# Dense coefficient spreads laid out by GpSimd, and the bias product as steps of the fold's bank rotation

## What is computed

```
x = x + layernorm(x) * scan(0.9, ctx * ctx)          # decayed running sum over tokens
h = layernorm(x) @ W_exp + b_exp                      # 512 -> 2048
h = butterfly(h, up_weights)                          # 11 stages of 2x2 pairs
h = gelu(h + up_bias)
h = butterfly(h, down_weights)
x = x + h @ W_con + b_con + down_bias                 # 2048 -> 512
```

## Time and profile before

| | us |
|---|---|
| median of 3 runs | 2771.31 (2770.5 to 2771.94) |
| profiled execution | 2771.06 |
| its span, first to last instruction | 2769.2 |
| PE busy | 2740.1 (99%) |
| DVE busy | 2122.9 (77%) |
| ACT busy | 1131.0 (41%) |
| GpSimd busy | 396.5 (14%) |

### The profile page before, as it was taken

How to read it: one execution, slowest core, us unless ns; L and a number is a source line. 1 busy time by engine, 2 the same in 40 slices (tenths; PEclk the granted TensorE clock), 3 DMA queues, 4 the chain that set the end, 5 groups by cost and what they waited for, 6 DMA issues and landing times.

```text
span 2769.2 us, 35072 instructions
## 1 busy us (share of the span) xinstructions
PE 2740.1 (99%) x12191; PEld 2260.4 (82%) x12191; DVE 2122.9 (77%) x3554; ACT 1131.0 (41%) x1715; POOL 396.5 (14%) x561
## 2 busy tenths in 40 slices
PE   8899999999999999999999999999999999999998
PEld 6778888888888888888888888888888888888887
DVE  9878787778878777787877878787787877778533
ACT  5743434334343433434343343434434343343432
POOL 4712011110201111010110101011020111102000
PEclk8999999999999999999999999999999999999999
DMA  9795765758576575856757585675857557584543
GB/s 275 266 294 152 216 191 167 228 154 240 165 204 203 168 213 155 255 163 195 201 170 223 155 239 168 190 214 162 235 152 224 185 175 223 161 243 152 182 149 99
DMA packets 292021, 540.48 MB, mean 195 GB/s; under 512 B 36918, under 2 KB 98518, under 8 KB 274950
## 3 DMA queue, kind: packets, MB, share of 16 engines
q1 hardware_dynamic: 285456, 535.77, 64.7%
q10 hardware_dynamic: 5414, 1.25, 0.3%
q0 software_dynamic: 976, 1.22, 0.2%
HBM read 445.83 MB, written 60.82 MB: 183 GB/s over the span
## 4 chain that ended last, share of the span: by engine, by line
PE 98%; ACT 1%; issue 0%; DVE 0%; DMA 0%; ACTq 0%
PE ps L1767 44%; PE ps L1788 25%; PE ps L1801 25%; PE ps L1664 1%; PE ps L1570 1%; PE ps L1642 0%; PE ps L1668 0%; ACT wcon L863 0%; PE ps L1662 0%; ACT w1r L885 0%; PE ps L1670 0%; PE ps L1868 0%; DMA wexp<-in_L_ffn_W_exp_dram 0%; PE ps L1716 0%; PE ps L1589 0%
## 5 line engine op out<-in xcount | busy, mean ns | idle before, releaser
L1767 PE MATMUL ps<-xop,w1r 128*128 128x512 f32 x5376 | 1364.1, 389 | 2.5 <-DVE xop L1296 1.6
L1767 PEld LDWEIGHTS ps<-xop,w1r 128*128 128x128 f32 x5376 | 1008.8, 188 | 212.7 <-DVE xop L1296 2.0
L1788 PE MATMUL ps<-w2r,ghi 128*128 128x512 f32 x2048 | 630.5, 389 | 0.0
L1801 PE MATMUL ps<-w2r,ghi 128*128 128x512 f32 x2032 | 625.8, 389 | 0.0
L1002 ACT ACTIVATE st<-ps 128x512 f32<-128x512 f32 x384 | 229.7, 598 | 839.9 <-PE ps L1767 839.9
L1403 DVE TENSOR_TENSOR x<-ps,x 128x512 f32<-128x512 f32 x508 | 348.6, 686 | 280.6 <-PE ps L1801 278.2
L1788 PEld LDWEIGHTS ps<-w2r,ghi 128*128 128x128 f32 x2048 | 384.4, 188 | 79.8
L1801 PEld LDWEIGHTS ps<-w2r,ghi 128*128 128x128 f32 x2032 | 381.2, 188 | 79.8 <-DVE glo L1426 0.4
L1421 DVE TENSOR_TENSOR g<-ps,st 128x512 f32<-128x512 f32 x384 | 262.9, 685 | 212.5 <-PE ps L1767 212.1
L1006 ACT ACTIVATE g<-g,gelu_bias 128x512 f32<-128x512 f32 x384 | 275.4, 717 | 362.7 <-DVE g L1421 361.6
L1426 DVE TENSOR_TENSOR glo<-g,ghi 128x512 fp32r<-128x512 f32 x510 | 347.5, 702 | 79.9 <-ACT ghi L1020 79.8
(11 more groups left out here) (174 smaller groups left out, 1701.8 us busy)
## 6 DMA issues: line engine op xcount, KB each, us to landing
w1r<-w_products SPq DMA_DIRECT2D x889, 256.0 KB, 3.3
w2r<-w_split SPq DMA_DIRECT2D x126, 1024.0 KB, 5.0
x<-in_x_dram SPq DMA_DIRECT2D x128, 256.0 KB, 7.2
raw<-kv SPq DMA_DIRECT2D x480, 64.0 KB, 2.2
out_dram<-x SPq DMA_DIRECT2D x120, 256.0 KB, 4.0
kv<-in_ctx_dram SPq DMA_DIRECT2D x64, 256.0 KB, 7.3
raw<-in_ctx_dram SPq DMA_DIRECT2D x64, 256.0 KB, 5.3
wexp<-in_L_ffn_W_exp_dram SPq DMA_DIRECT2D x4, 1024.0 KB, 10.9
```

The lines of the kernel that those rows point to most:

```text
L1767: last = nc.tensor.matmul(bank[:, :], w1r[:, slot, w, c * P:(c + 1) * P], xop[:, XPOS[m], v, c, :], start=(opens and i == 0), stop=(i == l ...
L1788: last = nc.tensor.matmul(ps_ya[j][:, :], g[:, p % 2, q, j * P:(j + 1) * P], w2r[:, p % 2, kk, w, :], start=(p == 0 and kk == 0 and i == 0 ...
L1801: last = nc.tensor.matmul(ps_yb[:, :], g[:, p % 2, q, j * P:(j + 1) * P], w2r[:, p % 2, kk, w, :], start=(kk == 0 and i == 0), stop=(kk == ...
```

## The change

It does four things. GpSimd lays the plain and the high coefficients of both sides side by side, one bit after the other (`dense_lows`, `dense_highs`: 4 and 8 copies for each side), and `stage_spread` reads those tiles. The bias turning and the bias product become the FOLD steps "bcol" (behind high_up 11) and "bias_low" (behind high_dn 3), with their evictions in ACT's order. On PE, the parted spreads of the down side go ahead of high_up, the top spread of the down side goes from behind high_up 9 to behind 8, and turn_low becomes plain transposes, its permutation moving into ACT's eviction. On ACT, `square(0, 1)` goes from behind high_up 6 to behind high_up 15, and `weights_hi(0)` gets a target of its own (`w1_first`), so that its wait for the bias product goes and a wait for its store comes in front of the tokens' evictions. On DVE, `high_products(0)` goes ahead of the first statistics.

```
+            def lay_dense(dst, src, order, ready):
+                half_n = dst.shape[1] // 2
+                v = src.rearrange(order, o=KH, a=2, b=2)
+                for bit in range(2):
+                    to = dst[:, bit * half_n:(bit + 1) * half_n]
+                    nc.gpsimd.tensor_copy(to.rearrange("q (o a l) -> q o a l", o=v.shape[1], a=2), v[:, :, :, :, bit])\
+                        .then_inc(ready, 1)
...
             nc.gpsimd.memset(parts_zero(1), 0.0).then_inc(parts_zeroed[1], 1)
+            dense_lows(0)
             load_high(pool, down_w, 1)
...
+            pool.wait_ge(sel_rounded, 2)
+            pool.wait_ge(top_sel_ready, 4)
+            dense_highs(0)
+            pool.wait_ge(fold_made, fold_at("low_up", 3) + 1)
+            dense_lows(1)
+            dense_highs(1)
...
             def weights_hi(n, groups=range(NG)):
                 if n == 0:
-                    act.wait_ge(bias_low, 1)
                     wait_kept(act, "high_up", R - 1)
...
             for r in range(R):
                 fold_step("high_up", r)
+                if r == R - 1:
+                    square(0, 1)
                 if r == 6:
-                    square(0, 1)
                     act.wait_ge(coef_spread, ALL_DONE)
...
-                if r == 13:
-                    act.wait_ge(bcol_turned, 1)
-                    act.activation(bcol, ps[4][:, 256:256 + 2 * KH], ACT.Copy).then_inc(bcol_kept, 1)
+                if r == 11:
+                    fold_step("bcol", 0)
...
-            for r in range(3, 8):
+            fold_step("high_dn", 3)
+            fold_step("bias_low", 0)
+            for r in range(4, 8):
                 fold_step("high_dn", r)
...
+            for group in range(2):
+                act.wait_ge(w1_stored[0][group], NX)
...
+            high_products(0)
             stats1(0, 0, xs[0], range(J))
-            high_products(0)
...
                     for bit in range(2):
                         last = nc.tensor.matmul(ps[bank][:, col:col + n // 2], sel[0:rows, choice, bit, :],
-                                                v[:, :, :, :, bit], start=(bit == 0), stop=(bit == 1))
+                                                dense[:, bit * (n // 2):(bit + 1) * (n // 2)],
+                                                start=(bit == 0), stop=(bit == 1))
...
-                        last = nc.tensor.matmul(o, LX[:, 1, 4 * i + c, :], rank_major(ident[:, :]), start=True, stop=True)
+                        last = nc.tensor.transpose(o, LX[:, 1, 4 * i + c, :], ident[:, :])
...
             spread_high(range(HIGH))
-            spread_low_dn(range(PARTED[0]))
+            spread_low_dn(range(LOWS))
             spread_high_dn(range(HIGH))
...
                 fold_step("high_up", r)
-                if r == 3:
-                    spread_low_dn(PARTED)
-                if r == 9:
+                if r == 8:
                     spread_top_dn((0, 1, 2, 3))
                 if r == 11:
-                    pe.wait_ge(path_product, ALL_DONE)
-                    pe.wait_ge(bias_loaded, 4 * NX)
-                    nc.tensor.transpose(ps[4][:, 256:256 + 2 * KH], bias_rows, ident[0:2 * KH, 0:2 * KH])\
-                        .then_inc(bcol_turned, 1)
+                    fold_step("bcol", 0)
...
                 fold_step("high_dn", r)
+                if r == 3:
+                    fold_step("bias_low", 0)
```

More of the change, by code:

```diff
@@ L103, in xattn_ffn_program @@
         W1f = sb("W1f", [P, KH, KD, P], stack=over)
-        sb("gap_wt", [P, 32 * P], stack=over)
+        w1_first = sb("w1_first", [P, 3, 2, 2 * P], f32r, stack=over)
+        sb("gap_wt", [P, 20 * P], stack=over)
         csrc_a = sb("csrc_a", [P, 32 * P], f32r, stack=over)
@@ L312, in xattn_ffn_program @@
         FOLD += [("low_up", k, "act") for k in range(KH)]
-        FOLD += [("high_up", r, "act") for r in range(R)]
+        FOLD += [("high_up", r, "act") for r in range(12)]
+        FOLD += [("bcol", 0, "act")]
+        FOLD += [("high_up", r, "act") for r in range(12, R)]
         FOLD += [("turn_high", q, "act") for q in range(R // 4)]
-        FOLD += [("high_dn", r, "act") for r in range(R - 3)]
+        FOLD += [("high_dn", r, "act") for r in range(4)]
+        FOLD += [("bias_low", 0, "act")]
+        FOLD += [("high_dn", r, "act") for r in range(4, R - 3)]
         FOLD += [("tokens", i, "act") for i in range(2)]
@@ L368, in spreads @@
             return dn * (LOWS + HIGH) + stage + 1
-        SPREAD_ORDER = (list(range(LOWS + HIGH)), [*range(PARTED[0]), *range(LOWS, LOWS + HIGH), *PARTED])
         def spread_count(dn, stage):
-            return dn * (LOWS + HIGH) + SPREAD_ORDER[dn].index(stage) + 1
+            return dn * (LOWS + HIGH) + stage + 1
         UP_DONE = LOWS + HIGH
@@ L407, in kept @@
                 return w1_columns(W1f, i), whole.rearrange("p (c k e) -> p c k e", c=KD, e=E)
+            if kind == "bcol":
+                return bcol, whole[:, 0:2 * KH]
+            if kind == "bias_low":
+                return yb, whole[:, 0:KH]
             if kind == "turn_high":
@@ L454, in w1_stage @@
                 return w1r[:, m0:m1, :, :]
+            if n == 0 and g < 2:
+                return w1_first[:, 2 * g:2 * g + m1 - m0, :, :]
             pos, first = ((6, 0), (6, 2), (4, 0))[g]
@@ L697, in choose, with dense_lows, dense_highs @@
                         .then_inc(sel_ready, 1)
+            def lay_dense(dst, src, order, ready):
[5 more added lines that the diff above has]
+                        .then_inc(ready, 1)
+            def dense_lows(dn):
+                pool.wait_ge(low_loaded[dn], LOW_LOADS * NX)
+                for stage in PLAIN:
+                    rows, off, n = src_place(stage)
+                    lay_dense(dense_low[dn][stage - PLAIN[0]][0:rows], low_src[dn][0:rows, off:off + n],
+                              "q (o l a b) -> q o a l b", dense_low_ready[dn])
+            def dense_highs(dn):
+                pool.wait_ge(high_loaded[dn], HIGH_LOADS * NX)
+                for b in range(HIGH):
+                    rows, off, n = src_place(b)
+                    lay_dense(dense_high[dn][0:rows, off:off + n], high_src[dn][0:rows, off:off + n],
+                              "q (l o a b) -> q o a l b", dense_high_ready[dn])
             def choose_high(b):
@@ L803, in _ @@
             pool.wait_ge(coef_loaded, NX)
-            pool.wait_ge(yb_kept, 1)
+            wait_kept(pool, "bias_low", 0)
             n = 0
@@ L1564, in spread, with stage_spread @@
             def spread(dn):
-                def stage_spread(src, place, stage, choice, order):
-                    rows, off, n = src_place(stage)
+                def stage_spread(dense, place, n, rows, choice):
                     bank, col = place
-                    v = src[0:rows, off:off + n].rearrange(order, o=KH, a=2, b=2)
                     for bit in range(2):
                         last = nc.tensor.matmul(ps[bank][:, col:col + n // 2], sel[0:rows, choice, bit, :],
-                                                v[:, :, :, :, bit], start=(bit == 0), stop=(bit == 1))
+                                                dense[:, bit * (n // 2):(bit + 1) * (n // 2)],
+                                                start=(bit == 0), stop=(bit == 1))
                     last.then_inc(coef_spread, 1)
@@ L1622, in low @@
                             pe.wait_ge(sel_ready, 2 * (LOWS - stage))
-                            stage_spread(low_src[dn], LOW_PLACE[stage], stage, HIGH + stage - PLAIN[0], "q (o l a b) -> q o a l b")
+                            rows, _, n = src_place(stage)
+                            pe.wait_ge(dense_low_ready[dn], 2 * (stage - PLAIN[0] + 1))
+                            stage_spread(dense_low[dn][stage - PLAIN[0]][0:rows], LOW_PLACE[stage], n, rows,
+                                         HIGH + stage - PLAIN[0])
                 def high(stages):
-                    pe.wait_ge(high_loaded[dn], HIGH_LOADS * NX)
+                    pe.wait_ge(dense_high_ready[dn], 2 * HIGH)
                     pe.wait_ge(sel_ready, 2 * (len(PARTED) + len(PLAIN) + HIGH))
@@ L1643, in fold_step @@
                         .then_inc(fold_made, 1)
+                    return
+                if kind == "bcol":
+                    pe.wait_ge(bias_loaded, 4 * NX)
+                    nc.tensor.transpose(bank[:, 0:2 * KH], bias_rows, ident[0:2 * KH, 0:2 * KH]).then_inc(fold_made, 1)
+                    return
+                if kind == "bias_low":
+                    wait_kept(pe, "bcol", 0)
+                    for k in range(KH):
+                        last = nc.tensor.matmul(bank[:, k:k + 1], LX[:, 0, k, :], bcol[:, k:k + 1], start=True, stop=True)
+                    last.then_inc(fold_made, 1)
                     return
@@ L1713, in _ @@
                 fold_step("turn_high", q)
[L1714 to L1717, removed]
             for r in range(R):
```

16 lines of the change are left out of this document (8 added, 8 removed).

## The result

The changed kernel takes 2775.55 us (median of 18 runs, 2773.98 to 2777.24); the kernel before took 2771.38 beside it (18 runs, 2770.5 to 2773.13). The ratio is 1.0014, with a 95% interval of 1.0008 to 1.0021: 4.2 us slower, by less than the 0.2% that the prediction took as its bound, but more than the interval allows for no change. The forecast was 2774 within 2769 to 2779. So the two profiles differ by 5.9 us where the medians differ by 4.2.

What follows compares the result with a forecast made beforehand. PE, busy 2740 of 2769 us, was taken as the bound, so only the prologue could move time. The square makes DVE 8.8 us late, 5.8 after recovery, 3.3 after slack: 2771.1 plus 3.3 gives 2774.4, stated as 2774, range 2769 to 2779.

Steps and rivals of the forecast that it cites:

- Part 1: PE's spreads on dense data: 8.9 us, ending at 51.6; PE then idles 4.6 us before the down side's top spread.
- d: DVE's total lateness from GpSimd's copies beside it, taken as 2 us, between 0 and 4.
- rival (a): Prologue: no clock fall at PE's wait, or DVE hardly late from copies; 2770 to 2772.5 us, chance 0.26 with rival (d).
- rival (d): PE's spreads: dense operands cost as much as strided ones, so the idle goes; 2772 us, chance 0.26 with rival (a).
- Part 2: GpSimd's copies beside DVE: 1.0 us lost at the first four, 1.1 in the down side's, together 2 us.
- Rival (c): GpSimd's copies lock DVE out entirely, making it over 4 us late; 2778 us, slower than 0.2%, chance 0.15.
- Part 3: End of high_up on PE: 79.3 us against 76.0 before, from a top spread at 68.0 plus clock loss.
- The 2.5 us charged: Clock loss on PE in high_up after over 5 us without work: 2.5 us, 0 to 3.4 taken.
- Part 4: ACT's square moved to high_up 15: DVE's scan of raw at 81.8, 8.8 us late, 3.3 after recovery and slack.
- the 2.5 us of slack: DVE's 2.47 us gap at 125.91, booked as room that cuts the lateness from 5.8 to 3.3 us.
- Part 5: turn_low as transposes, 7.19 to 1.99 us of PE, plus stepped eviction, bias product and store wait; booked as 0.
- (b): Prologue: PE's saved work arrives after all, about 10 us won, 2761 us; chance 0.09.

Runs made afterwards that it cites:

- e12: The changed kernel unchanged, run once more with a second profile; 2775.01 us, ratio 1.0014.
- e1: The changed kernel with only ACT's square(0, 1) put back behind high_up 6; 2771.7 us, ratio 1.0001.
- e4: The changed kernel with turn_low as 32 products with the permuted identity again and a plain eviction; 2775.4 us, ratio 1.0013.
- e11: e1, GpSimd's copies kept, with the parted spreads of the down side again behind high_up 3; 2771.34 us, ratio 0.9999.
- e10: The kernel before with two down-side low-part subtractions moved from DVE to GpSimd and ACT's first square ahead of low_up; 2773.21 us, ratio 1.0006.
- e2: The kernel before with only ACT's square(0, 1) moved behind high_up 15; 2775.0 us, ratio 1.0013.
- e7: The changed kernel with the square back at step 6, no GpSimd copies, and high_products(0) behind the first statistics again; 2770.41 us, ratio 0.9995.
- e9: e7 with the parted spreads of the down side again behind high_up 3; 2770.94 us, ratio 0.9997.
- e8: The changed kernel, square at step 6, no GpSimd copies, down-side low-part subtractions moved from DVE to GpSimd, first square ahead of low_up; 2772.53 us, ratio 1.0003.

## Why the prediction held, and where its steps were wrong

**Part 1, the dense spreads: wrong in size.** The forecast was 8.9 us from the high spread (up) to the end of the down side's; the rows give 14.2 (45.85 to 55.29 + 4.76). The step took the dense column price at full clock, 0.115 us, for all of them, although the text itself noted that the old spreads of the down side ran at half clock. At half clock dense and strided cost the same (4.76 and 4.83). At full clock the high spread took 2.58 and not 2.1. The clock fell at 49 to 50 us, in a stretch in which PE was busy without a gap, on products of few columns. PE was free for the top spread at 69.76 and not at 61.4: 3.1 us from the later start of the spreads, 5.3 from the spreads themselves. So it idled 0.46 us there and not the 4.6 named (6.6 with the forecast's own d of 2). That is what rival (a) named ("the spreads may themselves run at half clock, then PE idles less") and rival (d) in part.

**Part 2, the copies: about right in size, but d held two delays for which the working had no term.** DVE's low products of the down side end at 70.08, 69.74 and 68.36 in the changed kernel, e12 and e1, and at 70.30 and 70.62 in e4 and e11, which have the copies too. Against 66.02 that is late by 2.3 to 4.6, where d was taken as 2 within 0 to 4. Up to the start of low_up the lateness of the first three is 3.1, 2.4 and 0.8. In e1 it is about what DVE's lane copy loses beside GpSimd's first four (1.58 us against 0.68), near the 1.0 charged. In e12 the lane copy is equally slow, so most of the difference to e1 is clock: the low spread took 2.29 us in e1 and 2.90 in e12. In the changed kernel's first profile the coefficients also landed 2 us later. Behind the start of low_up the loss is 0.9, 1.3 and 1.5, against the 1.1 taken, although the down side's copies took 6.4 us and not 4.9. The timelines of GpSimd and DVE in the changed kernel:

```profile
31.42 5.74 POOL L715 COPY HX<-HX 64x32 f32<-64x32 f32 x8 [0.46 <-DMA HX<-in_L_ffn_up_weights_dram]
37.12 2.87 POOL L715 COPY WT<-wcon 16x128 f32<-16x128 f32 x4
39.95 3.55 POOL L715 COPY WT<-HX 64x32 f32<-64x32 f32 x8
```

```profile
36.71 1.54 DVE L1264 TENSOR_TENSOR_SCAN kvT<-decay,kvT 128x512 f32<-128x512 f32 x1
```

The scan stretched from 1.22 to 1.54, 0.32 lost in 1.54 or 21%, where the earlier trace rows gave 28%. Rival (c) called d over 4 decisive; three profiles have it (4.1, 4.3 and 4.6), all with the late landing, and the full lock it argued from did not come from the copies. It did come in e10, from longer GpSimd reads. A rule of the Trainium skill (SBUF — State Buffer, section "Who interferes with whom": whoever issues first has the shared ports for its whole instruction, and the other blocks) agrees with e10's copy of 4.40 us; in the changed kernel the scan's 21% beside short copies shows no such block.

**Part 3, the end of high_up: 78.75 measured, 79.3 forecast, for another reason.** The top spread started at 70.22 and not 68.0, because d was 4 and not 2; from there to turn_high it took 8.5 us, as the steps without the clock loss gave (2.1 + 6.4 + 0.25 = 8.8). The 2.5 us charged for a fall after the idle did not occur, as the idle was 0.46. Two errors of about 2 us cancelled, which is luck. That the clock can fall after an idle gap shows elsewhere: 1.00 before and 0.50 behind the 3.61 us before 120.39. This agrees with the Trainium skill, TensorE: Matmul & The Clock Gate, section "HAM oscillation — how this bites in real kernels"; the fall at 49 us, with PE busy throughout, is not what that section describes.

**Part 4, the square: right in mechanism, wrong in the slack behind it.** The scan of raw was forecast for 81.8 and came at 81.38; it was called the dearest line, and e1 and e2 show that it is nearly the whole of the difference. What DVE recovers: weights_lo(1) is 4.6 us late, where 5.8 was forecast. The 2.81 us wait is gone as said, and the scans beside GpSimd's sums gave back more than the 0.2 assumed. But then the lateness grew again, because GpSimd's sums, which used to wait for DVE, now stand beside its next rows. The timelines of DVE behind weights_lo(1), first in the kernel before, then in the changed one:

```profile
90.31 1.23 DVE L1202 TENSOR_TENSOR w1r<-stmp,w1r 128x1024 fp32r<-128x1024 f32 x1
...
92.43 1.23 DVE L1223 TENSOR_TENSOR_SCAN kvT<-decay,kvT 128x512 f32<-128x512 f32 x1
...
106.54 1.22 DVE L1202 TENSOR_TENSOR w1r<-stmp,w1r 128x1024 fp32r<-128x1024 f32 x1
```

```profile
95.15 1.74 DVE L1243 TENSOR_TENSOR w1r<-stmp,w1r 128x1024 fp32r<-128x1024 f32 x1
...
97.77 1.63 DVE L1264 TENSOR_TENSOR_SCAN kvT<-decay,kvT 128x512 f32<-128x512 f32 x1
...
112.65 1.22 DVE L1243 TENSOR_TENSOR w1r<-stmp,w1r 128x1024 fp32r<-128x1024 f32 x1
```

So lo(3) is 6.1 late. **The failed step is the 2.5 us of slack.** The gap of 2.47 was read as room on DVE that a later DVE uses up. It is the wait for ACT's xop, and ACT is itself tied to DVE: its weights_hi(5) waits until the result of DVE's weights_lo(3) is stored. The timelines of ACT in the kernel before and in the changed one:

```profile
114.28 1.08 ACT L885 ACTIVATE w1r<-stmp 128x1024 fp32r<-128x1024 f32 x1
```

```profile
118.79 1.06 ACT L923 ACTIVATE w1r<-stmp 128x1024 fp32r<-128x1024 f32 x1 [1.92 <-DMA w_products<-w1r]
...
123.53 0.60 ACT L902 ACTIVATE raw<-ps 128x512 f32<-128x512 f32 x1 [0.26 <-PE ps L1726]
```

Here ACT took up 1.6 of the 6.1, and then the store held it. PE stands idle the longer for that, 3.61 us before 120.39 where it was 1.59, and its products behind it run at half clock; ACT waits for them, as its second row shows, and 1.3 us are lost again. Behind that the gap travels with the chain (2.07 instead of 2.47). The forecast asked for each gap who ends it, but not whom that releaser follows. The first product of tokens is then 5.8 late in this profile and 5.0 in e12's, against 3.3 forecast; the medians of the timed runs say 4.2 and 3.5. Over all fourteen profiles lo(3) moves by 7.4 us and its distance to that product by 1.1, so there was never much slack to use.

**Part 5: right in its sum of 0.** turn_low's products took 2.2 us with PE waiting for ACT in between, the eviction in steps cost nothing that shows, and with the products back, in e4, the median moved by 0.15 us. That 0 is two terms, about 1 us won ahead of weights_hi(5) and about as much lost to the clock behind it, which the forecast did not have. The bias product took 3.63 us in its new place, at full clock, and not 4.83, and ACT waited 1.24 us for it; what that is worth no run tells apart. The wait for w1's stores left no row. Turn_high waits 1.63 us for ACT, forecast as 1.5 and hidden.

**The rivals.** (b), 2761, was wrong as argued: PE's work fell by 2.8 us and not one came through. (a), 2770 to 2772.5, described PE rightly but not DVE. The chance of 0.76 for "within 0.2%" was on the case that came, a ratio of 1.0014. The range held with room on both sides, but that the sum lies within 1.6 us is partly luck: DVE's lateness grew again between lo(1) and lo(3), most of the slack was not there, and against both stands a greater recovery at lo(1), 3.8 us and not 3.0, and a scan 0.4 us earlier than forecast.

**What stays open.** Why the clock near the start stays low for some 7 us in one execution (e1) and 10 in another (e12), with the same instructions, no run tells. Whether e7 beats the kernel before (by 1.0 us in the medians) its interval does not settle; that it beats the changed kernel, 2770.4 to 2775.5, is clear.

## What to carry to other kernels

Before booking a later start against a gap, follow the gap's releaser one step further back: if it waits, through a store or another engine, for the very work that is late, the gap moves along, and only what the releaser can catch up until that wait binds is slack (here 1.6 us, of which 1.3 were lost again). A step off the bottleneck engine (ACT's square, 1.9 us) can cost more than every saving on the busiest one, if the engine that sets the pace waits for it. And price small products at the clock at which they will run: dense operands gained 1.3 us of 3.9 at full clock and 0.1 of 4.8 at half.

## What was not expected of the hardware

The granted clock fell while PE was busy without a gap: in the kernel before, at 49 us in the changed one, at 45 in e7, at 48 in e9, each time during the spreads. In all of them it was back only in a stretch that begins between 59 and 63, inside high_up. A copy of 128x16 on DVE took 4.40 us beside a GpSimd subtraction that reads SBUF (0.17 without it), and a scan 3.46 (1.22). The landing of the first coefficients varied between executions: by 13.7 us in nine of the fourteen profiles, between 15.3 and 15.8 in five (changed, e4, e8, e10, e11), with the same instructions ahead of it in all.
